# A decoder block's delta-rule inverses in two halves: a new order of work on all engines

## What is computed

```python
q, k, v = silu_conv(x @ Wq), silu_conv(x @ Wk), silu_conv(x @ Wv)
beta = sigmoid(x @ Wb)
q, k = l2norm(q), l2norm(k); v, kb = v * beta, k * beta
# for each sequence, head and chunk of 32 tokens:
inv = -(kb @ k.T) * strict_lower
for i in range(1, 32):
    inv[i, :] += inv[i, :] @ inv
u, w = (inv + I) @ v, (inv + I) @ kb
# over the 4 chunks in order: o = q S + (q k.T * lower) (u - w S);  S += k.T (u - w S)
short, long = conv(v, fir_short), conv(v, fir_long)          # 5 and 64 taps
stats = head_stats of short, long, o, v                      # mean, variance, |.|, norm
p = softmax(gelu([x, stats] @ Wg1 + bg1) @ Wg2 ...)          # 4 weights per token
o = p-mixture of the four;  o *= sigmoid(gelu([x, stats of o, v] @ Wog1) @ Wog2)
x = layernorm(x + rmsnorm(o) @ Wo)
x = layernorm(x + xattn(x, ctx)); x = layernorm(x + experts(x))
```

## Time and profile before

| | us |
|---|---|
| median of 3 runs | 472.37 (471.81 to 473.17) |
| the profiled execution | 472.83 |
| its span, first to last instruction | 471.1 |
| TensorE busy, VectorE busy, ScalarE busy | 350.7, 317.4, 152.0 |
| GpSimd busy | 37.4 |
| mean granted TensorE clock | 0.841 |
| chain that ended last, by engine | VectorE 40%, TensorE 38%, issue 12%, DMA 4%, ScalarE 4% |

### The profile page before, as it was taken

One profiled execution on the slowest core, in us unless ns is written; L12 is line 12 of the kernel. 1 busy time (PEld: TensorE's weight loads), 2 busy tenths in 40 slices (PEclk: granted clock), 3 DMA queues, 4 the chain that ended last, 5 costly groups with the idle time before them and its releaser, 6 DMA issues.

```text
span 471.1 us, 8238 instructions
## 1 busy us (share of the span) xinstructions
PE 350.7 (74%) x2912; PEld 239.2 (51%) x2912; DVE 317.4 (67%) x1049; ACT 152.0 (32%) x267; POOL 37.4 (8%) x74
## 2 busy tenths in 40 slices
PE   3978985968952468343374998979989799878992
PEld 2544553768940456111243556565566555655672
DVE  3046567768999825966536957668876788777535
ACT  1232332223354335222030442224422343314240
POOL 6000000007940000000000000000000000000000
PEclk9999998579966556655567899998999989998997
DMA  7670110299625500000010000000200000000000
GB/s 215 193 196 25 22 22 0 53 287 245 179 69 115 111 4 5 0 1 0 0 46 1 22 1 0 24 0 1 68 1 22 0 0 22 0 1 1 24 1 22
DMA packets 51601, 23.54 MB, mean 50 GB/s; under 512 B 18248, under 2 KB 51056, under 8 KB 51312
## 3 DMA queue, kind: packets, MB, share of 16 engines
q1 hardware_dynamic: 35056, 14.71, 12.5%
q10 hardware_dynamic: 16512, 8.39, 7.0%
HBM read 18.77 MB, written 3.28 MB: 47 GB/s over the span
## 4 chain that ended last, share of the span: by engine, by line
DVE 40%; PE 38%; issue 12%; DMA 4%; ACT 4%; DVEq 1%; SPq 0%; ACTq 0%; POOL 0%
PE bank L484 6%; PE bank L706 5%; PE bank L714 5%; DVE prod L1458 4%; DVE inv L1460 4%; PE bank L459 3%; DVE as_t L1438 3%; DVE nt L1162 3%; DVE nt L1163 3%; PE bank L478 2%; DVE as_t L1260 2%; PE bank L511 2%; DVE as_t L1251 2%; DMA early<-blocks 2%; DVE sm L1164 2%
## 5 line engine op out<-in xcount | busy, mean ns | idle before, releaser
L714 PEld LDWEIGHTS bank<-w_sb,as_t 128*128 128x128 f32 x512 | 61.1, 194 | 22.9 <-issue 18.8
L1018 ACT ACTIVATE as_t<-bank,cb 128x512 f32<-128x512 f32 x64 | 43.3, 686 | 76.1 <-PE bank L706 60.8
L714 PE MATMUL bank<-w_sb,as_t 128*128 128x128 f32 x512 | 63.9, 280 | 5.0 <-ACT as_t L1018 5.0
L706 PE MATMUL bank<-as_t,w_sb 128*128 128x512 f32 x128 | 66.6, 648 | 0.0
L1438 DVE SCALAR_TENSOR_TENSOR as_t<-bank,as_t 128x128 f32<-128x128 f32 x128 | 36.0, 344 | 23.4 <-PE bank L714 21.1
L459 PE MATMUL bank<-ident,as_t 128*128 128x128 f32 (+1 forms) x64 | 12.1, 319 | 33.9 <-DVE as_t L1260 15.7
L484 PE MATMUL bank<-wtap,xc_pad 128*128 128x384 f32 x96 | 35.5, 509 | 0.0
L706 PEld LDWEIGHTS bank<-as_t,w_sb 128*128 128x128 f32 x128 | 24.1, 207 | 20.2 <-issue 18.8
L1229 DVE TENSOR_TENSOR as_t<-bank,masks 128x512 f32 (+1 forms) x32 | 20.0, 686 | 17.2 <-PE bank L511 17.2
L459 PE MATMUL bank<-ident,early 128*128 128x128 f32 x96 | 17.2, 309 | 17.7 <-DVE early L1208 6.0
L459 PEld LDWEIGHTS bank<-ident,as_t 128*128 128x128 f32 (+1 forms) x64 | 7.4, 145 | 42.1 <-DVE as_t L1260 17.3
(11 more groups left out here) (217 smaller groups left out, 614.1 us busy)
## 6 DMA issues: line engine op xcount, KB each, us to landing
toep<-taps_back ACTq DMA_DIRECT2D x8, 1024.0 KB, 8.6
toep<-x SPq DMA_DIRECT2D x8, 256.0 KB, 2.7
early<-x SPq DMA_DIRECT2D x4, 256.0 KB, 3.6
w_sb<-w SPq DMA_DIRECT2D x1, 1024.0 KB
w_sb<-w SPq DMA_DIRECT2D x2, 512.0 KB
blocks<-as_t SPq DMA_DIRECT2D x16, 64.0 KB, 2.0
early<-blocks SPq DMA_DIRECT2D x1, 1024.0 KB, 8.0
src<-vb SPq DMA_DIRECT2D x16, 64.0 KB, 6.5
```

The source lines that it names most:

```text
L706: pe.matmul(ps[4 + half][:, :], w1_sb[:, e, half * 128:half * 128 + 128], x2_c.rearrange("p b t -> p (b t)"), start=True, stop=True).then_ ...
L714: last = pe.matmul(bank(6 + e % 2)[:, b, :], hid[:, e % 2, half, b * L:(b + 1) * L], w2_sb[:, e, half, :], start=(half == 0), stop=(half = ...
L1018: act.activation(hid[:, e % 2, half, :], ps[4 + half][:, :], ACT.Relu, bias=c_of("b1", 2 * e + half)).then_inc(s["hid_ready"], 1)
```

## The change

The 64 pairs are split in two halves of 32: half 0 is the first two groups of sequences. Each half has its own block and inverse transfers, with one block per partition. GpSimd recurses half 0 alone and starts when group 1's blocks have landed; VectorE recurses half 1 alone, all rows. The substitution runs per half, the context's keys and values, and later the first group's gate chain, are put between its steps. Sums for the statistics are made for group 0 first and for the others later; their moments are worked in two calls, over 64 columns for group 0 and 192 for the rest, in place of five. v is written where it is kept by a silu of its own, so that GpSimd's copy goes. `products` of both halves of a group come before the next group's last projection. The Toeplitz tables have four buffers, two of them the space of the expert weights, which are loaded later. ScalarE's small constants are made before the FIR. A layernorm's inverse root is one `pow` by GpSimd. Bank numbers of the first group's chain move. The diff follows, cut to its core, engine by engine. SyncE:

```diff
+            def half_in(f):
+                sp.wait_ge(blocks_out, 16 * NC * 2 * (f + 1))
+                sp.dma_start(blk[f].rearrange("p j i -> p (j i)"),
+                             blocks_dram[HP * f:HP * f + HP].rearrange("r n j i -> (r n) (j i)")
+                             ).then_inc(blocks_in[f], 16)
+                sp.wait_ge(s["vb_ready"], 2 * (f + 1) + credit["vb_ready"])
+                for n in range(NC):
+                    for c in range(4):
...
+            def inverses_of(f):
+                sp.wait_ge(s[f"solved{f}"], 1)
...
+                sp.wait_ge(inverse_out[f], 16)
+                for n in range(NC):
+                    for c in range(4):
...
+            for g in range(1, NG):
+                sp.wait_ge(s["xt_ps"], g)
+                sp.dma_start(x_g[:, :, :], x[g * G:g * G + G].rearrange("b t c -> t b c")).then_inc(x_in, 16)
+                if g == NG - 1:
+                    blocks_of(0)
+            blocks_of(1)
+            half_in(0)
+            blocks_of(2)
+            blocks_of(3)
...
+            half_in(1)
...
+            inverses_of(0)
             sp.wait_ge(s["fir_ps"], CHUNKS)
+            sp.dma_start(c_g, ctx_in[0:G].rearrange("b t c -> t b c")).then_inc(ctx_loaded, 16)
...
+            inverses_of(1)
```

GpSimd; the product and the difference of each column j are two instructions on `n` times `m` elements:

```diff
-            with pool.Fori(0, NG) as g:
-                pool.wait_ge(s["silu_ready"], (g + 1) * G)
-                pool.tensor_copy(src[:, bass.ds(g * G, G), 3, :], qkv_g[:, :, 2 * D:3 * D]).then_inc(s["v_kept"], 1)
...
+            for j in range(CH - 1):
+                n, m = CH - 1 - j, j + 1
+                p = prod_pool[:, 0:m * n].rearrange("p (c i) -> p c i", c=m)
...
+            def layernorm_root(count):
+                pool.wait_ge(root_asked, count)
+                pool.tensor_tensor(out=sm2[:, 0:G], in0=sm1[:, 0:G], in1=neg_half[:, :], op=ALU.pow
+                                   ).then_inc(root_done, 1)
...
+            pool.wait_ge(s["stats_ready"], 1)
             stats_of(0)
+            layernorm_root(1)
+            pool.wait_ge(s["stats_ready"], 2)
+            stats_of(1)
+            layernorm_root(2)
+            layernorm_root(3)
```

TensorE, in `project_step` and behind the FIR:

```diff
                 project(g, 1)
+                products(g - 1, 0)
                 project(g, 2)
-                products(g - 1, 0)
+                products(g - 1, 1)
                 project(g, 3)
-                products(g - 1, 1)
...
+            solve_blocks(0, 0)
             ct(0)
             xat(0)
+            apply_solved(0, 1)
+            solve_blocks(0, 1)
             values(0)
+            apply_solved(0, 2)
+            solve_blocks(0, 2)
+            pe.wait_ge(s["xac_ready"], 1)
             keys(0)
...
+            apply_solved(0, 3)
+            solve_blocks(0, 3)
+            pe.wait_ge(s["u_ready"], NC * 4)
+            delta_products(0)
+            delta_products(1)
+            pe.wait_ge(s["kr_ready"], 1)
+            delta_transposed(0)
+            pe.wait_ge(vs_in[1], 16 * NC * 4)
+            solve_blocks(1, 0)
+            delta_transposed(1)
+            apply_solved(1, 1)
+            solve_blocks(1, 1)
+            apply_solved(1, 2)
             st_transposed(0)
             source_gate(0)
+            solve_blocks(1, 2)
+            apply_solved(1, 3)
+            pe.wait_ge(s["delta_ready"], 1)
             source_logits(0)
-            pe.wait_ge(s["delta_ready"], NG)
+            solve_blocks(1, 3)
+            pe.wait_ge(s["u_ready"], 2 * NC * 4)
+            delta_products(2)
+            delta_products(3)
+            delta_transposed(2)
+            delta_transposed(3)
+            pe.wait_ge(s["lmax_ready"], 1)
             st2_transposed(0)
```

ScalarE:

```diff
-                act.activation(qkv_g[:, b, :], pr[:, 0:NQKV], ACT.Silu).then_inc(s["silu_ready"], 1)
+                act.activation(qk_g[:, b, :], pr[:, 0:2 * D], ACT.Silu)
+                act.activation(src[:, bass.ds(g * G + b, 1), 3, :].rearrange("p a c -> p (a c)"), pr[:, 2 * D:3 * D],
+                               ACT.Silu).then_inc(s["silu_ready"], 1)
...
             st_columns(0)
             source_gate(0)
+            keep_solved(1, 2)
+            keep_solved(1, 3)
+            act.wait_ge(inverse_out[1], 16)
+            keep_delta(2)
+            keep_delta(3)
             source_exp(0)
```

VectorE, in `layernorm` and from the end of the projections:

```diff
-                own(dve.tensor_scalar(sm1[:, 0:G], mv[:, :, 1], EPS, None, ALU.add))
-                rsqrt(sm2[:, 0:G], sm1[:, 0:G], G)
+                dve.tensor_scalar(sm1[:, 0:G], mv[:, :, 1], EPS, None, ALU.add).then_inc(root_asked, 1)
+                roots[1] += 1
+                dve.wait_ge(root_done, roots[0] + roots[1])
...
+            sums(3, 0, B, 1)
...
+            dve.wait_ge(blocks_in[1], 16)
+            invert(0, 24)
+            residual(0, 1)
+            invert(24, CH - 1)
+            dve.sem_inc(s["solved1"], 1)
+            residual(0, 2)
+            sums(0, 0, G, 2)
+            residual(0, 3)
+            sums(1, 0, G, 3)
...
             rotate_keys(0)
+            delta(0)
             source_sums(2, 0, G, 4)
+            residual(1, 1)
+            source_moments(0, G)
+            residual(1, 2)
+            sums(0, G, B, 2)
+            residual(1, 3)
+            delta(1)
...
             mixture_stats(0)
+            delta(2)
+            delta(3)
+            sums(1, G, B, 5)
             gated(0)
+            source_sums(2, G, B, 6)
             x1_norm(0)
+            source_moments(G, B)
```

More of the change, by code:

```diff
@@ L314, in _, with blocks_of @@
             sp.dma_start(taps_back, long_taps[:, 1, :]).then_inc(long_out, 16)
[L315 to L319, removed]
+            def blocks_of(g):
                 sp.wait_ge(s["gram_kept"], 2 * H * (g + 1) + credit["gram_kept"])
@@ new lines, in solve_blocks @@
+            def solve_blocks(f, n):
+                pe.wait_ge(inverse_in[f][n], 16 * 4)
+                if n:
+                    pe.wait_ge(s["r_ready"], f * (NC - 1) + n)
+                elif f:
+                    pe.wait_ge(s["u_ready"], NC * 4)
+                for r in range(PQ):
+                    for c in range(4):
+                        rows = slice(CH * c, CH * c + CH)
+                        last = pe.matmul(ps[c][rows, r * DH:(r + 1) * DH], inv_t[rows, f, n, r, :],
+                                         vs[rows, f, n, r // H, r % H * DH:(r % H + 1) * DH],
+                                         start=True, stop=True)
+                last.then_inc(s["d_ps"], 1)
@@ new lines, in delta_products, with delta_transposed @@
+            def delta_products(g):
+                for r in range(GP):
+                    last = pe.matmul(ps[O_BANKS[g]][r % H * DH:r % H * DH + DH, r // H * L:(r // H + 1) * L],
+                                     u[:, GP * g + r, :], as_t[:, GP * g + r, 1, :], start=True, stop=True)
+                last.then_inc(s["o_ps"], 1)
+            def delta_transposed(g):
+                pe.wait_ge(s["oc_ready"], g + 1)
+                transposes(OT_BANKS[g], o_c[:, g, :, :]).then_inc(s["ot_ps"], 1)
@@ L1480, in _, with sums, invert @@
-            dve.sem_inc(s["sums_ready"], 1)
-            source_moments(1, 0, B)
+            def sums(k, a, b, squares_ready):
+                source_sums(k, a, b, squares_ready)
+                dve.sem_inc(s["sums_ready"], 1)
+            def invert(first, last):
+                for j in range(first, last):
+                    n, m = CH - 1 - j, j + 1
+                    p = prod[:, 0:m * n].rearrange("p (c i) -> p c i", c=m)
+                    own(dve.tensor_tensor(out=p, in0=blk[1][:, j, j + 1:].unsqueeze(1).broadcast_to([128, m, n]),
+                                          in1=wide(inv[:, 1, 0:m, j], n), op=ALU.mult))
+                    own(dve.tensor_tensor(out=inv[:, 1, 0:m, j + 1:], in0=inv[:, 1, 0:m, j + 1:], in1=p,
+                                          op=ALU.subtract))
```

514 lines of the change are left out of this document (235 added, 279 removed).

## The result

The changed kernel takes 458.77 us (median of 4 runs, 455.93 to 462.97), the kernel before 472.09 beside it: a ratio of 0.970, 95% interval 0.965 to 0.976. The forecast was 445.0 in a range of 433 to 459. So the sign held, but the median lies only 0.2 us inside the range's upper end: the change brings some 14 us (15.9 between the profiled executions, 472.83 and 456.92 us), half of the 27 forecast. One of the four runs, the one of 462.97 us, was slower as a whole, at a mean clock of 0.850 against 0.862 to 0.865.

A forecast was written before the change was run, and what follows sets the result against it. No single engine bounds the kernel; between FIR and loop, 105 us, engines take turns. Gains of 16.0 us up to the queries and 11.5 from roots, 27.5 in all, gave 445 us, range 433 to 459.

The forecast's parts named there:

- Projections, +4.8: Projections, up to the FIR: longer cycles and GpSimd contention, less the last group's gain of 1.1, add 4.8 us.
- the products in the cycle: Projections: products moved ahead of the last projection now stand in each group's cycle, 3 times 1.07 = 3.2 us.
- the silu split: Projections: one more fixed ScalarE cost per group, about 0.17 us, 0.7 in all.
- GpSimd's company: Last group's norms: some 14 two-input VectorE instructions stretch by 1.4 beside GpSimd's recursion, +2.0 us.
- Exclusion in the projections: First rival: GpSimd and VectorE alternate by whole instructions, +6 in place of +2, 450 us; chance 0.17 with the last rival.
- FIR, -6.5: Long FIR: four table buffers remove waits of 4.22 and 1.57 us and 0.7 us of slow clock.
- Inverses: GpSimd's half 67 to 109 us, under the FIR; VectorE's 23 us from near 109; costs nothing, by a small margin.
- Middle: Between FIR and loop: substitution from 132.0, with group 0's gate chain between its steps, x1 at 216.7 us.
- Moments after x1: Loop start: 6.5 us of moments after x1 delay TensorE's queries, ending at 227.5 against 243.5; a wait of 5 us.
- Roots, 11.5: Layernorms: power taken as 0.5 us, each root saves 1.35 us, 10 x 1.35 x 0.85 = 11.5 us.
- TensorE fills the loop: Loop, within the rival that roots bring nothing (or pow takes 1.9 us): 456.5 us; chance 0.14.
- TensorE warms up: Rival: half 1 beside the gate chain lifts the clock from 0.50, 10 us less, 435 us; chance 0.10.

The follow-up runs named there:

- the tables on SyncE: Changed kernel, but third and fourth Toeplitz table issued by SyncE behind group 2's x load instead of by ScalarE: 453.38 us, ratio 0.959.
- the old products: Changed kernel with third and fourth table issued by SyncE and second products and masks in their order before the change: 447.44 us, ratio 0.947.
- the repaired kernel with VectorE's roots: Changed kernel with two tables on SyncE, old product order, contexts and exponential earlier, moments of groups 2 and 3 later, layernorm roots on VectorE: 461.61 us, ratio 0.977.

## Why the prediction was right, and where it failed

**Projections, +4.8: failed, by one term.** The first FIR matmul came 14.9 us later than before. 9.6 of that is the issue of the third and fourth table, which the prediction put nowhere: it counted these loads as waits removed from the FIR and never as instructions of ScalarE, though group 0's squares stood behind them in the listing. What it did price came to 5.3, the last group's gain taken off. Inside that: the products in the cycle 1.26 us a group (forecast 1.07), the silu split about nothing (16.72 us a cycle against 16.65; forecast 0.17), GpSimd's company 2.6 (forecast 2.0).

**Exclusion in the projections.** The forecast took a share, and the first rival whole instructions. The rows after show whole instructions: a short VectorE instruction ends when GpSimd's ends, and the next gets in first. The Trainium skill states it so (SBUF — State Buffer, Who interferes with whom: the ports that VectorE and GpSimd share are an exclusive lock, and the order of issue decides who is blocked), and this trace agrees for the short instructions with two inputs, 0.51 to 0.55 us in place of 0.19. The mechanism was the rival's, the size nearer the forecast's (2.6 measured, 2.0 against the rival's 6), since only every second instruction waits. Three instructions with one input grew as well, to 0.60, 0.70 and 0.62 us where they took 0.17 to 0.18 without GpSimd. The long ones of the kernel before stay open: a step took 0.92 us there, where 0.62 for VectorE (the prediction's price) and the 0.60 us that GpSimd's 220 elements take at 103.60 us in the kernel after, one behind the other, would be 1.22.

**FIR, -6.5:** right in kind, no table wait is left; from its first matmul to the substitution 35.8 us, 1.7 less than forecast.

**Inverses:** GpSimd needed 39.4 us (42 forecast), VectorE's first 24 columns 19.3 us (19), and it idled before the residual. Both started late, GpSimd at 75.1 us (67 forecast), VectorE at 124.3 (109), 5 us more than the projections' delay: half 1's blocks left SyncE only at 115.7. It cost nothing, as said: TensorE solved half 1's first blocks at 162.04 without a wait.

**Middle:** x1 add came 82.7 us behind the first solve, forecast 80.4. The contexts behind sixteen loads in SyncE's queue were not in the sum; they cost 2.2 us in the kernel after and 4.2 with the tables on SyncE.

**Moments after x1:** a wait of 4.43 us where 5 was said, and the queries 15.7 us behind x1 add (15.1). Right.

**Roots, 11.5: the number held by luck, its reason did not.** From the queries to the end the walk is 216.5 us, 11.1 less than before. But the power takes 1.01 us, not 0.5, a root saves 0.87 us, not 1.35, and the roots alone in the kernel before bring 7.2 us on that stretch. That is what the prediction's own product gives with the measured root, 10 x 0.87 x 0.85 = 7.4. The other 3.9 go with TensorE's clock, 1.00 in two steps where it was 0.94 and 0.97, and stood in no term. "TensorE fills the loop" fell; so did "TensorE warms up" in the place it named: the middle's clock rose from 0.50 only to 0.65 and 0.53, and the middle took 2.3 us more than the sum.

**The sum.** The profiled end is 11.6 us behind the forecast's 443.6: projections 10.1, FIR -1.7, middle 2.3, moments 0.6, walk 0.4. Had the issue been in the sum, it would have said 454.6; with the root's true size too, 458.7. So the range held through its width, and its middle failed by the issue and, hidden by the clock, by the power's price.

## What to carry to other kernels

Price a DMA as an instruction of the engine that issues it, above all several large ones in a row, and look at what is due on that engine behind them. Take time out of a chain that TensorE waits on before rearranging work around it: here twelve short roots brought 20 us on top of the new order, which without them made the kernel slower as first written and brought 11 us repaired. And measure such changes together as well as alone: the same roots brought 7 us in the old order. A move that feeds another engine early is only worth its place in a cycle if that engine would otherwise be late: GpSimd could start 9.8 us later at no loss.

## What was not expected of the hardware

- An issue of a 1 MB transfer on ScalarE took 0.40 us as the first, 1.5 to 1.9 as the second, and 2.3 to 5.0 as the third and fourth of a row. On SyncE, behind ScalarE's two, the third took 0.57 us and the fourth 4.82. What it waits for no run shows.
- GpSimd's power of 128x4 elements took 1.01 us twelve times over, where a copy of 128x16 took 0.20.
- A slow stretch of TensorE's clock lasts through full work: 7.62 us busy of 8.00 at 0.50. Such stretches lasted 3 to 13 us. Some followed waits of TensorE of 1 us or more, as the one above; but in the walk's second step three began behind a wait of only 0.40 us, at 304.4 us in the kernel before, at 284.0 with the old products, at 298.8 in the kernel after with VectorE's roots, and in the kernel after the same wait, at 296.0, had none behind it. The kernel after had none between 258 and 450 us, the repaired kernel with VectorE's roots three between 294 and 393. That the roots are worth 20 us and not 7 goes with this clock; that shorter waits keep it up was not tried by itself, and these rows don't bear it out. Why the third step there took 70.17 us in one profile, and whether it does so in each run, stays open; its four runs lay between 460.35 and 462.78.
- Ahead of the same 37 of 64 matmuls of one `apply_solved` TensorE stood 0.7 to 2.0 us in four kernels, with nothing in the profile that it waits for. It was not looked into.
